# Attention layer on one core: in four of 16 tiles half the maxima from a + relu(b - a), and v's product in halves

## The reference

```
xn  = layernorm(x)
out = x + attention(xn, w_qkv, w_out) + ffn(xn, w_gate, w_up, w_down)

attention: 16 heads of 16 features; q, k = rope(q), rope(k)
           scores = q k^T / 4;  attn = softmax(scores);  out = (attn v) w_out^T
ffn:       (silu(xn wg^T) * (xn wu^T)) wd^T, integer weights / 127, 768 hidden
```

## Time and profile before

| | |
|---|---|
| median of 3 runs | 3136.37 us (3134.51 to 3140.29) |
| the profiled execution | 3135.18 us |
| its span, first to last instruction | 3133.4 us |
| mean granted TensorE clock | 0.984 |
| PE busy | 2966.5 us, 95% |
| DVE busy | 2816.9 us, 90% |
| ACT busy | 2412.5 us, 77% |
| POOL busy | 430.3 us, 14% |

### The profile page before, as it was taken

The page is one execution under the profiler, slowest core; times in us unless marked ns, Lnnn a source line. Parts: engine busy times, 40 slices in busy tenths (PEclk is TensorE's granted clock), DMA queues, the critical chain, the costliest instruction groups (busy, mean ns, idle before and its releaser), DMA issues.

```text
span 3133.4 us, 51833 instructions
## 1 busy us (share of the span) xinstructions
PE 2966.5 (95%) x19736; PEld 899.2 (29%) x19736; DVE 2816.9 (90%) x3214; ACT 2412.5 (77%) x4609; POOL 430.3 (14%) x672
## 2 busy tenths in 40 slices
PE   5888988799999999999999999999999999999999
PEld 3555555122222222222222222222222222222225
DVE  6777776999999999999999999999999999999962
ACT  4454444488888888888888888888888888888873
POOL 3445454000000000000000000000000000000000
PEclk8999999799999999999999999999999999999999
DMA  2222222011111111111111111111111111111125
GB/s 95 82 88 86 95 87 84 16 30 29 29 30 29 29 30 29 29 30 29 30 29 29 29 29 29 29 29 29 29 29 29 29 29 29 29 29 29 29 62 169
DMA packets 124540, 136.14 MB, mean 43 GB/s; under 512 B 43265, under 2 KB 103297, under 8 KB 124289
## 3 DMA queue, kind: packets, MB, share of 16 engines
q1 hardware_dynamic: 124288, 132.79, 15.3%
HBM read 88.15 MB, written 34.08 MB: 39 GB/s over the span
## 4 chain that ended last, share of the span: by engine, by line
PE 84%; DVE 6%; POOL 3%; ACT 3%; issue 2%; DMA 0%; SPq 0%; POOLq 0%; DVEq 0%
PE psum L691 33%; PE psum L707 30%; PE psum L656 14%; PE psum L566 2%; PE psum L639 2%; POOL qk_rot L862 2%; PE psum L589 2%; DVE row_max L1211 1%; ACT probs L817 1%; POOL parts L868 1%; DVE y_blk L1132 1%; ACT silu L761 1%; ACT staged L768 1%; DVE rot_s L1110 1%; DVE stats L945 1%
## 5 line engine op out<-in xcount | busy, mean ns | idle before, releaser
L1211 DVE TENSOR_REDUCE row_max<-psum 128x1 f32<-128x1024 f32 x2048 | 2409.8, 1219 | 65.4 <-PE psum L656 41.8
L817 ACT ACTIVATE probs<-psum 128x512 f32<-128x512 f32 x4096 | 2129.7, 602 | 343.3 <-PE psum L707 333.1
L707 PE MATMUL psum<-q_op,k_op 51*128 51x512 f16 x4096 | 1236.6, 383 | 43.2 <-ACT probs L817 20.2
L691 PE MATMUL psum<-probs,v_op 128*32 128x512 f32 x8192 | 1093.0, 605 | 9.0
L656 PE MATMUL psum<-k_op,q_op 48*128 48x512 f16 x4096 | 1033.2, 388 | 21.9 <-DVE row_max L1211 20.2
L707 PEld LDWEIGHTS psum<-q_op,k_op 51*128 51x128 f16 x4096 | 311.1, 94 | 1356.2 <-ACT probs L817 1251.2
L930 POOL TENSOR_TENSOR acc_sb<-acc_sb,inv_rows 128x512 f32<-128x512 f32 x64 | 81.7, 1277 | 1807.3 <-DMA inv_rows<-inv_dram 1807.3
L656 PEld LDWEIGHTS psum<-k_op,q_op 48*128 48x128 f16 x4096 | 213.5, 93 | 316.8 <-DVE row_max L1211 313.6
L691 PEld LDWEIGHTS psum<-probs,v_op 128*32 128x32 f32 x8192 | 163.0, 108 | 260.8 <-issue 260.1
L754 ACT ACTIVATE parts<-qk_rot 128x512 f16<-128x512 f32 x64 | 40.3, 630 | 236.3 <-POOL qk_rot L862 236.3
L566 PE MATMUL psum<-xnT,w 128*128 128x512 f16 x768 | 188.1, 393 | 6.9 <-DVE h L1123 6.9
(11 more groups left out here) (102 smaller groups left out, 1021.4 us busy)
## 6 DMA issues: line engine op xcount, KB each, us to landing
qk_dram<-staged SPq DMA_DIRECT2D x64, 256.0 KB, 3.3
q_op<-qk_dram SPq DMA_DIRECT2D x128, 128.0 KB
k_op<-qk_dram SPq DMA_DIRECT2D x128, 128.0 KB
x_ln<-in_x SPq DMA_DIRECT2D x16, 512.0 KB, 4.1
x_res<-in_x SPq DMA_DIRECT2D x16, 512.0 KB, 5.0
y_dram<-y_blk SPq DMA_DIRECT2D x16, 512.0 KB, 3.2
k_op<-qk_dram SPq DMA_DIRECT2D x128, 64.0 KB
q_op<-qk_dram SPq DMA_DIRECT2D x128, 64.0 KB
```

The lines of the kernel that those rows point to most:

```text
L691: mm = pe.matmul(bank(7)[32 * j:32 * j + 32, :], v_op[:, h % 2, t, :], probs[:, g3 % 2, j * BANK:(j + 1) * BANK], start=(t == 0), stop=(t ...
L707: pe.matmul(bank(b), k_op[r:e, h % SLOTS, t * P:(t + 1) * P], q_op[r:e, h % SLOTS, j * BANK:(j + 1) * BANK], start=True, stop=True).then_i ...
L817: nc.scalar.activation(probs[:, g2 % 2, j * BANK:(j + 1) * BANK], bank(b), ACT.Exp, scale=to_score).then_inc(s2_used, 1)
L1211: nc.vector.tensor_reduce(row_max[:, hl % 2, t, half:half + 1], psum[:, 2 * half * BANK:(2 * half + 2) * BANK], AX.X, ALU.max).then_inc(s1 ...
```

## The change

Five things change, all in the second stage.

1. For some halves (c, half), listed in `diffs`, the maximum over 1024 keys is made in another way. With a the scores of the first 512 keys and b those of the second, max(a, b) = a + relu(b - a). These are both halves of tiles 2 to 15 of the first head (28) and half 1 of tiles 4, 9, 12 and 15 of each other head (63 x 4 = 252), 280 in all.
2. In the step before, PE makes b - a in one bank of the exponentials' ring: two matmuls of 512 columns on the upper row half, one with k's second 512 keys, one with the negated first 512 (k_neg), accumulated. ACT takes its positive part into `over` (SBUF, two buffers). In the tile's own step PE makes only a, and DVE makes a + over and its maximum in one instruction (tensor_tensor_reduce).
3. POOL negates the needed columns of k for each head (`negate`), one head ahead.
4. v's product runs two steps behind the exponentials instead of one (probs has three buffers), and is cut into two halves of 256 columns each: one after s1, ahead of the difference and of the half-1 maxima, one at the end of the step, after s3. For a head's first tile there is only the second place, with all 512 columns. s2 and s3 now stand together behind the half-1 maxima. SAVE_AT and INV_AT move by one step, and the second stage has one step more.
5. The transpose of the maxima counts as one item of the ring instead of two; the number of items before a step comes from a table. Offsets that were always zero here (`+ ... * i`) are gone.

```diff
+LOWEST = -3.0e38
+DIFF_TILES = (4, 9, 12, 15)
+DIFF_FROM = 2
+PV_LAG = 2
+PROBS = PV_LAG + 1
...
-    probs = sb(sB, "probs", [P, 2, TILES * P])
+    probs = sb(sB, "probs", [P, PROBS, TILES * P])
...
+    k_neg = sb(sB, "k_neg", [P, 2, 2, BANK], F16)
+    over = sb(sB, "over", [P, 2, BANK])
...
-    SAVE_AT = FIRST2 + TILES + 1
+    SAVE_AT = FIRST2 + TILES + PV_LAG
...
-    STAB_ITEMS = 2
...
+    diffs = [(c, half) for c in range(DIFF_FROM, TILES) for half in range(2)]
+    diffs += [(TILES * h + t, 1) for h in range(1, HEADS) for t in DIFF_TILES]
+    diff_number = {at: d for d, at in enumerate(diffs)}
+    def diff_halves(c):
+        return [half for half in range(2) if (c + 1, half) in diff_number]
+    def stab_items(c):
+        return 1 if head_of(c, STAB_AT) is not None else 0
+    def score_items(c):
+        return 4 if 0 <= c - FIRST2 < N1 else 0
+    ring_items = [0]
+    for c in range(STEPS_B):
+        ring_items.append(ring_items[c] + stab_items(c) + score_items(c) + len(diff_halves(c)))
...
# max_half, PE
-            for j in range(2):
+            for j in range(1 if (c, half) in diff_number else 2):
...
# weigh_v, PE
-                    pe.wait_ge(s2_used, items_before(c - 1) + extra_items(c - 1) + 4 + HEAD_ITEMS * SLOTS * i)
+                    if t == 0 and part == 0:
+                        return
...
+                    if t == 0 or part == 0:
+                        pe.wait_ge(s2_used, items_before(c - PV_LAG + 1))
+                    n0, n1 = (0, BANK) if t == 0 else (part * (BANK // 2), (part + 1) * (BANK // 2))
                     for j in range(4):
-                        mm = pe.matmul(bank(7)[32 * j:32 * j + 32, :], v_op[:, h % 2, t, :], probs[:, g3 % 2, j * BANK:(j + 1) * BANK],
-                                       start=(t == 0), stop=(t == TILES - 1), tile_position=(0, 32 * j))
+                        mm = pe.matmul(bank(7)[32 * j:32 * j + 32, n0:n1], v_op[:, h % 2, t, :],
+                                       probs[:, g3 % PROBS, j * BANK + n0:j * BANK + n1],
+                                       start=(t == 0), stop=(t == TILES - 1 and part == 1), tile_position=(0, 32 * j))
...
+            def difference(at, half, item):
+                h, t = divmod(at, TILES)
+                pe.wait_ge(neg_ready, h + 1)
+                b = take_bank(item)
+                q_tile = q_op[HALF:HALF + ROWS, h % SLOTS, t * P:(t + 1) * P]
+                n0 = (2 * half + 1) * BANK
+                pe.matmul(bank(b), q_tile, k_op[HALF:HALF + ROWS, h % SLOTS, n0:n0 + BANK], start=True, stop=False)
+                pe.matmul(bank(b), q_tile, k_neg[HALF:HALF + ROWS, h % 2, half, :],
+                          start=False, stop=True).then_inc(s2_full, 1)
             for j in range(4):
-                if j == 2 and c < N1:
-                    max_half(c, i, 1)
-                if j == 3:
-                    weigh_v(g2 - 1)
+                if j == 2:
+                    weigh_v(0)
+                    for half in diff_halves(c):
+                        difference(c + 1, half, item)
+                        item += 1
+                    if c < N1:
+                        max_half(c, i, 1)
...
+            weigh_v(1)
...
# step, ACT
+            def positive_part(at, half, item):
+                d = diff_number[at, half]
+                if d >= 2:
+                    before_at, before_half = diffs[d - 2]
+                    act.wait_ge(s1_used, 2 * before_at + before_half + 1)
+                b = arrived(item)
+                nc.scalar.activation(over[:, d % 2, :], bank(b), ACT.Relu).then_inc(s2_used, 1)
             g2 = c - FIRST2
-            if 0 <= g2 < N1:
-                if g2 >= 2:
-                    act.wait_ge(pv_done, g2 - 1 + UNROLL * i)
-                for j in range(4):
+            if PROBS <= g2 < N1:
+                act.wait_ge(pv_done, g2 - PROBS + 1)
+            for j in range(4):
+                if j == 2:
+                    for half in diff_halves(c):
+                        positive_part(c + 1, half, item)
+                        item += 1
+                if 0 <= g2 < N1:
...
# POOL
+        def negate(h):
+            pool.wait_ge(qk_loaded[h % SLOTS], 16 * QK_LOADS * (h // SLOTS + 1))
+            if h >= 2:
+                pool.wait_ge(s1_full, 2 * TILES * (h - 1))
+            halves = k_op[:, h % SLOTS, :].rearrange("p (a b n) -> p a b n", a=2, b=2)
+            first = 0 if h == 0 else 1
+            nc.gpsimd.tensor_scalar(k_neg[:, h % 2, first:2, :], halves[:, first:2, 0, :], -1.0, None,
+                                    ALU.mult).then_inc(neg_ready, 1)
+        negate(0)
         for h in range(HEADS):
             copy_v(h)
+            if h + 1 < HEADS:
+                negate(h + 1)
             split_max(h, h == 0)
...
# step, DVE
+                    d = diff_number.get((c, half))
+                    if d is not None:
+                        dve.wait_ge(s2_used, diff_item(c, half) + 1)
+                        nc.vector.tensor_tensor_reduce(over[:, d % 2, :], bank(2 * half), over[:, d % 2, :], 1.0, LOWEST,
+                                                       ALU.add, ALU.max, row_max[:, hl % 2, t, half:half + 1]).then_inc(s1_used, 1)
+                        continue
```

More of the change, by code:

```diff
@@ L316, in sequence_of, with items_before, diff_item @@
         return n
[L318 to L328, removed]
+    diffs = [(c, half) for c in range(DIFF_FROM, TILES) for half in range(2)]
[10 more added lines that the diff above has]
+        ring_items.append(ring_items[c] + stab_items(c) + score_items(c) + len(diff_halves(c)))
+    def items_before(c):
+        return ring_items[c]
+    def diff_item(c, half):
+        g = c - 1
+        return ring_items[g] + stab_items(g) + score_items(g) // 2 + diff_halves(g).index(half)
     def run_steps(step):
@@ L665, in take_bank @@
                 if item >= RING:
-                    pe.wait_ge(s2_used, item - RING + 1 + HEAD_ITEMS * SLOTS * i)
+                    pe.wait_ge(s2_used, item - RING + 1)
                 return 4 + item % RING
@@ L672, in step @@
             if h is not None:
-                pe.wait_ge(stab_step, STAB_STEPS * (h + 1 + SLOTS * i))
+                pe.wait_ge(stab_step, STAB_STEPS * (h + 1))
                 b = take_bank(item)
                 pe.transpose(bank(b).bitcast(F16)[:, 0:P], stab[:, :, :].rearrange("p a t -> p (a t)"),
-                             identh[:, :]).then_inc(s2_full, STAB_ITEMS)
-                item += STAB_ITEMS
+                             identh[:, :]).then_inc(s2_full, 1)
+                item += 1
@@ new lines, in weigh_v @@
+                    if part == 1:
+                        mm.then_inc(pv_done, 1)
+            def difference(at, half, item):
[7 more added lines that the diff above has]
+                          start=False, stop=True).then_inc(s2_full, 1)
@@ L792, in step, with arrived @@
             item = items_before(c)
-            def arrived(item, n=1):
-                act.wait_ge(s2_full, item + n + HEAD_ITEMS * SLOTS * i)
+            def arrived(item):
+                act.wait_ge(s2_full, item + 1)
                 return 4 + item % RING
@@ L806, in step @@
                 if h >= 1:
[L807 to L810, removed]
-            g2 = c - FIRST2
-            if 0 <= g2 < N1:
-                if g2 >= 2:
-                    act.wait_ge(pv_done, g2 - 1 + UNROLL * i)
-                for j in range(4):
+                    act.wait_ge(stab_loaded, 32 * (h))
+                b = arrived(item)
+                nc.scalar.activation(stabT[:, :], bank(b).bitcast(F16)[0:STAB_PARTS * TILES, 0:P], ACT.Copy).then_inc(s2_used, 1)
+                item += 1
+            def positive_part(at, half, item):
[3 more added lines that the diff above has]
+                    act.wait_ge(s1_used, 2 * before_at + before_half + 1)
+                b = arrived(item)
+                nc.scalar.activation(over[:, d % 2, :], bank(b), ACT.Relu).then_inc(s2_used, 1)
+            g2 = c - FIRST2
+            if PROBS <= g2 < N1:
[4 more added lines that the diff above has]
+                        positive_part(c + 1, half, item)
+                        item += 1
+                if 0 <= g2 < N1:
                     b = arrived(item)
-                    nc.scalar.activation(probs[:, g2 % 2, j * BANK:(j + 1) * BANK], bank(b), ACT.Exp,
+                    nc.scalar.activation(probs[:, g2 % PROBS, j * BANK:(j + 1) * BANK], bank(b), ACT.Exp,
                                          scale=to_score).then_inc(s2_used, 1)
```

35 lines of the change are left out of this document (17 added, 18 removed).

## The result

| | before | after |
|---|---|---|
| median | 3136.44 us (8 runs) | 3146.53 us (8 runs, 3142.49 to 3149.47) |
| ratio, with its 95% interval | | 1.0035 [1.0025, 1.0045] |
| the profiled execution's span | 3133.4 us | 3147.7 us |
| first matmul of the maxima to the first neg_max | 36.8 us | 34.6 us |
| a head, neg_max to neg_max: most heads | 38.89 us | 38.98 us |

The change makes the kernel 10 us slower (0.35%); 3100 was forecast. The time lies inside the range, on the other side of "no change". In the profiled executions, from neg_max 1 to neg_max 63, the 62 heads take 2419.1 us instead of 2411.4: +7.7, where the forecast had -33. Eight of the 62 heads take 0.25 to 0.28 more than the others, since one of their steps is that much longer; what does that is open.

What follows compares the result with a forecast made beforehand. A three-bank PE-ACT loop of 2.39 us a step was taken to bound the kernel, PE at 2.24 after; heads 38.36 against 38.89. 3135.2 - 33 (heads) - 5 (start) + 3 (end) = 3100 us, range 3000 to 3170.

Steps and rivals of the forecast that it cites:

- the loop s3, exponential, s2, product: Fourth score matmul, its exponential, third score matmul of the next step, v's product: 2.39 us a step, to be broken.
- plain step: Step with no difference, transpose or head's product start: PE-bound at 2.24 us instead of 2.39, a gain of 0.15 each.
- rival B: Halves carry no second entry and exit: PE's plain step 1.99, DVE bounds at 2.262; 2965 us, chance 0.17.
- C: Rival: each half product dearer, its short pass not hiding the weight loads; 3197 us at 0.05 each, chance 0.18.
- D: Rival: the relu reloads ACT's table, two loads of 1.28 us for each of 280 relus; +500 or more, chance 0.05.
- Each difference costs 0.43 and returns nothing: Two extra PE matmuls in the step before the tile cost 0.43 us; DVE's saved time is unused while PE bounds.
- the end: 19 steps with scores but no maxima pay the second entry and exit, one product more follows: taken as +3 us.
- the start: First head's differences save 7.7 to 12 us, POOL's clearing and negation cost 3.5: net taken as -5 us.
- ACT's copy of the accumulator ends before s0's exponential at 0.64: In the step where a head's product starts, the copy delays no first score exponential; that step takes 2.61 us.
- the making step: Step before tiles 4, 9, 12 and 15, where PE makes the difference: 2.24 + 0.43 = 2.67 us, four a head.
- 1.29, just before 1.33: In a plain step, s0's bank comes free for s3 at 1.29 us, before PE reaches s2 and s3 at 1.33.
- the step of the transpose: Step with the transpose of the maxima: s1 waits for a bank until 0.65 instead of 0.22, making 2.67 us.

Runs made afterwards that it cites:

- experiment 3: Kernel before the change with v's product still whole between s2 and s3, but two steps behind, the transpose as one ring item, no differences: 3128.5 us.
- experiment 1: The changed kernel without any difference and without POOL's negations, v's product in halves two steps behind: 3029.3 us, ratio to before 0.964.
- experiment 6: The changed kernel with each difference made by one matmul, from k's second half minus first stored by POOL, instead of two: 3141.7 us.

## Why the prediction was wrong

**What held.** The kernel before is bound by the loop s3, exponential, s2, product, and the change breaks it: experiment 3 against 1. A visit of the product costs PE nearly the same beyond its streaming for 256 columns as for 512. Its length is 1.00 for 512 and 0.57 for 256, so 0.43 for each 256 columns and 0.14 that both have, and some 0.10 stands ahead of it both times. A plain step came out at 2.25, with PE's pieces as forecast and not rival B's 1.99. The runs show the size of this fixed part and not its cause: 0.57 for a half product, of which about 0.43 goes with the columns.

The streaming times that the forecast subtracted agree with the distance of starts. At a granted clock of 1.00, 16 fp16 matmuls of 512 columns start 0.216 apart, (3.62 - 0.38)/15 in the first stage of the kernel before, against its 0.213:

```profile
302.81 3.62 PE L566 MATMUL psum<-xnT,w 128*128 128x512 f16 x16
```

At 0.50 they start 0.427 apart in the changed kernel (549.82 to 552.80, eight starts), and the two passes of a whole product in the kernel before 0.853 (587.38 and 588.24), twice that. 512 columns in 0.427 are 1.2 a ns and in 0.216 2.37 a ns, which is what the traces show of the 1.2 and 2.4 GHz; the clock's records hold the shares 0.50 and 1.00 alone.

The mechanisms of rivals B, C and D did not come: the kernel is slower, as C had it, but the passes of a half start 0.24 apart (1506.65 and 1506.89) and a half lasts 0.57, so the halves are not dearer. The relu's record is 0.598 long, and the second stage loaded the exponential's table once, 1.28 us, in a stage with 280 relus. "Each difference costs 0.43 and returns nothing" was right in its sign and near in its size; the runs give 0.49.

**Where the sum failed.** A head was to take 38.36 and most took 38.98: 0.62, over 62 heads 38 us, and the eight slow heads make it 41. That is most of the 49 us between 3100 and the profiled execution's 3147.7 + 1.8; the end has 4 of them, the start 3, and the first stage, whose code is the same, 2.

- The step named wrongly: "ACT's copy of the accumulator ends before s0's exponential at 0.64". My own table had the last exponential of the step before start at 2.24, so ACT is free only at 0.48 of the next; the copy ran from 0.47, s0's exponential from 0.95, s3 waited for it until 1.62, and the step took 2.94 instead of 2.61. 0.33 a head, 20 us, the largest term of the error. By this sum the kernel would be some 10 us faster than before without it.
- The wait left out: the ring was not checked for the making step. By "ACT starts at 0.64, 1.13" s1's bank would have come free at 1.78, which gives PE's 2.67 once more. But s1's exponential started at 1.20 and its bank was free at 1.84, because s0's exponential starts 0.48 after its matmul (1506.35 to 1506.83 in the plain step), where rows 4 have 0.42 for s3. 0.06 in each making step, 0.24 a head, 15 us. The same 0.06 uses up the room in "1.29, just before 1.33": s3 came at 1.35 in the plain step. What the 0.06 is stays open. It is not ACT being busy: in the last steps ACT is idle for 1.02 us ahead of s0's exponential (3091.17), and that still starts 0.49 after its matmul. s0's exponential has one wait more ahead of it, for the old product; a kernel without that wait was not tried.
- Ten plain steps of 2.247 instead of 2.24: 0.07 a head, 4 us; the step of the transpose 0.03 shorter than forecast.
- The end: +7.1, not +3. The last head's three rows of maxima land later, beside the loads of y: PE waits 4.2 us for them, 1.5 before. And a step with both a product and a projection takes 3.09 instead of 2.91, for the last dozen steps with scores. The kernel of experiment 3, with the product whole, waits 4.0 us at the same place and has steps of 2.91, so the halves cause the second part alone. Why the rows land later is open.
- The start: -2.3, not -5. POOL's clearing ended at 546.6 instead of 543.5, since it waits for a store of the first stage, and the negation of 1024 columns took 2.82, not 1.6; PE waited 5.15 for it. When that store lands differs from run to run: in the kernel with the first head's differences alone the clearing ended at 543.3. The steps behind it took 1.71, as forecast.

**What was right for a reason that was not.** The 0.43 of a making step was priced as PE's two matmuls. The ring asks for more by itself: 0.22 + 0.48 + 0.50 + 0.64 + 0.32 + 0.57 = 2.73, and experiment 6 shows that it, not PE, is the bound. It was luck that the wrong bound gave nearly the right step; for the kernel of experiment 6, with one matmul, it failed by the whole amount, 55 us.

**What the forecast could have said.** By the same table a head without differences comes to 14 x 2.24 + 2.67 + 2.61 = 36.6, and the working said in so many words that a difference returns nothing; but the parts were only summed, and the gain of the one was not held against the loss of the other. The net of -0.53 was made of -2.25 for the halves and +1.72 for the differences. Measured by most heads (37.03 in experiment 1) they are -1.86 and +1.95. With errors of 0.39 and 0.23 in its terms so small a net had no sure sign; 0.70 for faster was too much.

## What to carry to other kernels

With a ring of n banks, write down for every item the time from its matmul to the start of the one n items on, and add PE's longest gap between two items in its order: that is a bound of its own beside every engine's busy time (2.39 a step in the kernel before, where DVE's reductions want 2.262), and a long operation is best cut in two where it lies between two items (2.39 to 2.25 here). An item more in the ring costs what the ring asks even if the engines have room (0.49 here, with two matmuls or one). Moving work to relieve an engine pays only while that engine bounds; price each part of a change by itself and compare the parts, since a small net of two large terms has the sign of their errors.

## What the runs showed of the hardware

- At a granted clock of 1.00, a visit of the product on four column groups lasts 1.00 us for 512 columns and 0.57 for 256, with about 0.10 more ahead of it: some 0.25 us do not shrink with the columns.
- The add-and-max over 512 columns from PSUM and SBUF is a record of 0.68 and an accumulator read of 0.08; two in a row start 0.68 apart (553.69 and 554.37, the first's read at 554.30), against 1.131 from start to start for the reductions of 1024 columns in the kernel before.
- POOL's negation of 1024 fp16 columns took 2.82 us, of 512 1.49.
- At a granted clock of 1.00, a bank comes free 0.64 to 0.65 after its exponential has started, and an exponential that finds ACT free starts 0.42 after its matmul (1508.06 to 1508.48 in the kernel before), or 0.48 for the first of a step (1506.35 to 1506.83 in the changed one).
